# Own orders for the first and last slots of a software pipeline of four graph layers

## The reference

```python
x = layernorm(x + edge(x))       # relu(A[i] + (C - A)[j]) with A = C - b = adj @ x, maximum over i: in effect a shift by relu(max(adj @ x) + b)
x = layernorm(x + gat(x))        # h = x W; scores leaky_relu(s1 + s2) * adj; softmax; att @ h + beta h; elu
x = layernorm(x + gcn(x))        # (adj @ x) W2 + bias
x = layernorm(x + attention(x))  # 8 heads of 64, q, k, v with biases, masked where adj == 0, softmax
```

## Time and profile before

| | us |
|---|---|
| median of 3 runs (2518.87 to 2520.77) | 2519.57 |
| the profiled execution, its own time | 2517.59 |
| its span, first to last instruction | 2515.7 |
| PE busy in the span | 2433.5 (97%) |
| DVE busy | 2216.3 (88%) |
| POOL busy | 1477.2 (59%) |
| ACT busy | 1333.6 (53%) |

### The profile page before, as it was taken

One profiled execution on the slowest core, in us unless ns is written; L12 is line 12 of the kernel. 1 busy time (PEld: TensorE's weight loads), 2 busy tenths in 40 slices (PEclk: granted clock), 3 DMA queues, 4 the chain that ended last, 5 costly groups with the idle time before them and its releaser, 6 DMA issues. The chain is left out here.

```text
span 2515.7 us, 55083 instructions
## 1 busy us (share of the span) xinstructions
PE 2433.5 (97%) x15509; PEld 2071.0 (82%) x15509; DVE 2216.3 (88%) x6934; ACT 1333.6 (53%) x4104; POOL 1477.2 (59%) x1806
## 2 busy tenths in 40 slices
PE   4899999999999999999999999999999999999995
PEld 3688888888888888888888888888888888888874
DVE  6889889989889889889889989999999999999974
ACT  3355555555555555555555555555555555555543
POOL 5655566566565565566566566566566565665641
PEclk9899999999999999999999999999999999999997
DMA  4265665665665665666666666666666666666564
GB/s 130 48 138 132 142 146 130 143 144 133 142 143 137 141 143 137 142 139 138 141 139 139 140 139 141 139 138 142 138 138 142 138 139 141 139 141 138 126 137 103
DMA packets 1375069, 341.01 MB, mean 136 GB/s; under 512 B 1078576, under 2 KB 1339312, under 8 KB 1375024
## 3 DMA queue, kind: packets, MB, share of 16 engines
q1 hardware_dynamic: 1375024, 340.47, 59.4%
HBM read 173.35 MB, written 166.99 MB: 135 GB/s over the span
## 5 line engine op out<-in xcount | busy, mean ns | idle before, releaser
L928 PE MATMUL rot<-w_hi,y_hi 128*128 128x512 f32 x1024 | 416.0, 406 | 2.8 <-DVE y_lo L842 2.1
L930 PE MATMUL rot<-w_hi,y_lo 128*128 128x512 f32 x1024 | 403.8, 394 | 0.0
L929 PE MATMUL rot<-w_lo,y_hi 128*128 128x512 f32 x1024 | 402.3, 393 | 0.0
L517 ACT ACTIVATE probs<-score,sc_nmax 128x128 f32<-128x128 f32 x1024 | 362.3, 370 | 27.3 <-DVE sc_nmax L682 24.2
L387 POOL TENSOR_TENSOR ve<-mv,eps_col 128x1 f32<-128x1 f32 (+1 forms) x448 | 130.9, 292 | 342.6 <-DVE mv L674 245.9
L420 POOL TENSOR_TENSOR x2b<-x,bias 128x512 f32<-128x512 f32 x128 | 166.1, 1298 | 264.1 <-DVE x L786 264.1
L682 DVE CUSTOM_DVE_ANT_0 score<-score,mask 128x128 f32<-128x128 f32 x1024 | 259.7, 315 | 1.3 <-PE score L1027 1.3
L704 DVE CUSTOM_DVE_ANT_0 dot_tmp<-x,u 128x512 bf16<-128x512 f32 x256 | 244.9, 992 | 11.9 <-ACT x L626 7.4
L430 POOL TENSOR_SCALAR e<-e 128x512 f32<-128x512 f32 x128 | 246.5, 1925 | 13.6 <-ACT e L577 13.6
L395 POOL TENSOR_TENSOR rs<-ve,half_neg 128x1 f32<-128x1 f32 (+1 forms) x448 | 249.5, 571 | 0.6
L415 POOL TENSOR_TENSOR x<-x,o_norm 128x512 f32<-128x512 f32 x128 | 165.8, 1295 | 141.4 <-DVE o_norm L740 141.4
(11 more groups left out here) (129 smaller groups left out, 7057.4 us busy)
## 6 DMA issues: line engine op xcount, KB each, us to landing
pt_hbm<-probs SPq DMA_DIRECT2D x508, 128.0 KB, 2.8
probs_t<-pt_hbm SPq DMA_DIRECT2D x127, 512.0 KB, 4.0
x_in<-in_x SPq DMA_DIRECT2D x128, 256.0 KB, 4.0
xt_hbm<-x_b SPq DMA_DIRECT2D x512, 64.0 KB, 2.3
xt_f<-xt_hbm SPq DMA_DIRECT2D x128, 256.0 KB, 2.8
out_x<-x SPq DMA_DIRECT2D x128, 256.0 KB, 2.5
ot_hbm<-o_t SPq DMA_DIRECT2D x508, 64.0 KB, 1.9
o_norm<-ot_hbm SPq DMA_DIRECT2D x127, 256.0 KB, 2.7
```

The costliest lines, as they stand in the source:

```text
L517: ins = act.activation(probs[:, 0, c, t, :], score_tile(c, g, h), ACT.Exp, bias=sc_nmax[:, c, t:t + 1], scale=-1.0, accum_out=sc_sum[:, pa ...
L928: pe.matmul(outp, lh, rh, start=first, stop=False)
L929: pe.matmul(outp, lh, rl, start=False, stop=False)
L930: return pe.matmul(outp, ll, rh, start=False, stop=last)
```

## The change

`slots` now takes three orders for each engine: `fill` for slots 0 to 7, `emit` (as before in slots 8 to 127, but for the points below) and `drain` for slots 128 to 135.

```diff
-def slots(eng, emit):
-    for s in range(WARM):
+def slots(eng, fill, emit, drain):
+    for s in range(FILL):
+        fill(Slot(s - s % BUFS, s % BUFS))
+    for s in range(FILL, WARM):
         emit(Slot(s - s % BUFS, s % BUFS))
     with eng.Fori(0, (LOOP_END - WARM) // BUFS) as turn:
...
-    for s in range(LOOP_END, SLOTS):
+    for s in range(LOOP_END, GRAPHS):
         emit(Slot(s - s % BUFS, s % BUFS))
+    for s in range(GRAPHS, SLOTS):
+        drain(Slot(s - s % BUFS, s % BUFS))
```

**Weights' lower parts on DVE**, in slots 1 to 5, in four instructions of 128 x 512 spread over the slot:

```diff
+            def lower_weight(slot, k):
+                n = slot.number() - 1
+                dve.wait_ge(w_hi_done, n + 1)
+                return dve.tensor_tensor(weights[w_order[n]][1][:, k, :], stage[n][:, k, :],
+                                         weights[w_order[n]][0][:, k, :].bitcast(F32), ALU.subtract)
```

**Edge product** of slots 0 to 7 in one plain fp32 product, without ACT's x_hi and POOL's x_lo:

```diff
+            def edge_product(slot):
+                buf = slot.buf(L_EDGE, 4)
+                if slot.fills():
+                    pe.wait_ge(x_loaded[buf], (slot.graph(L_EDGE) - buf) * 4 + 16)
...
+                if slot.fills():
+                    return pe.matmul(rot[0][:, :], adj_t[:, :], x_in[:, buf, :], start=True, stop=True)
+                return three(rot[0][:, :], (adj_t_hi[:, :], adj_t_lo[:, :]), (x_hi[:, :], x_lo[:, :]), True, True)
```

**Drain order of PE**, with PV's wait and PV now apart (the products between them cut to their names):

```diff
+            def drain(slot):
+                if slot.on(L_PV):
+                    if slot.last(L_PV):
...
+                    else:
+                        slot.wait(pe, pt_in, L_PV, each=16)
+                if slot.on(L_GAT):
...
+                if slot.on(L_QK) and not slot.last(L_QK):
...
+                    projection(q_bank, "wq", slot).then_inc(q_mm, 1)
+                if slot.on(L_ATT):
...
+                if slot.on(L_QK) and not slot.last(L_QK):
...
+                    projection(k_bank, "wk", slot).then_inc(k_mm, 1)
+                if slot.last(L_QK - 1):
...
+                    projection(late_q_bank, "wq", slot.after(), True).then_inc(q_mm, 1)
...
+                    ins.then_inc(score_mm, 1)
+                if slot.last(L_QK - 1):
...
+                    projection(late_k_bank, "wk", slot.after(), True).then_inc(k_mm, 1)
+                if slot.on(L_PV):
+                    first = slot.buf(L_PV, BUFS) // GROUP * GROUP
...
+                    ins.then_inc(pv_mm, 1)
```

More of the change, by code:

```diff
@@ L56 @@
 SLOTS = GRAPHS + L_OUT
+WEIGHTS = 5
 class Slot:
@@ L327, in emit @@
                     buf = slot.buf(L_LOAD, 4)
-                    slot.wait(sp, x_lo_done, L_LOAD, 4)
+                    slot.wait(sp, edge_mm, L_LOAD, 4)
                     slot.wait(sp, x1_done, L_LOAD, 4)
                     load(slot.graph(L_LOAD), buf)
[L333 to L338, removed]
                 if slot.on(L_TR):
@@ L360, in emit @@
                                      x4[:, first + g, :]).then_inc(out_stored[g], 16)
-            slots(sp, emit)
+            slots(sp, fill, emit, drain)
             for g in range(GROUP):
@@ L459, in emit @@
                         .then_inc(out_shift_done, GROUP)
-                if slot.on(L_EDGE) and not slot.on(L_QK):
-                    add_eps(slot, "0", L_EDGE)
-                    power(slot, "0", L_EDGE)
-                low_x(Slot(slot.base, slot.offset + 1))
+                if slot.after().on(L_EDGE) and not slot.after().fills():
+                    low_x(Slot(slot.base, slot.offset + 1))
                 if slot.on(L_GAT):
@@ L478, in emit @@
                     power(slot, "2", L_GCN)
-                for n in range(len(w_order)):
-                    if slot.first(n):
-                        split_weight(n)
                 if slot.on(L_V):
@@ L497, in _ @@
+            slots(pool, fill, emit, drain)
         @block.scalar
@@ L551, in emit @@
                 if slot.on(L_QK):
+                    if slot.first(L_QK):
+                        act.wait_ge(const_in, 16 * 4)
                     slot.wait(act, q_mm, L_QK)
@@ L595, in emit @@
                         half.then_inc(half_exp, 1)
-                round_x(Slot(slot.base, slot.offset + 1))
-                for n in range(1, len(w_order)):
-                    if slot.first(n - 1):
-                        split_weight(n)
+                if slot.after().on(L_EDGE) and not slot.after().fills():
+                    round_x(Slot(slot.base, slot.offset + 1))
                 if slot.on(L_QK):
@@ L638, in _ @@
+            slots(act, fill, emit, drain)
         @block.vector
@@ L923, in _ @@
+            slots(dve, fill, emit, drain)
         @block.tensor
@@ L952, in _, with projection @@
             y2 = [a[:, :].rearrange("p (k n) -> p k n", k=KC) for a in (y2_hi, y2_lo)]
-            def projection(banks, w, slot):
+            def projection(banks, w, slot, late=False):
                 w_hi, w_lo = weights[w]
@@ L960, in projection @@
                     cols = slice(chunk * P, (chunk + 1) * P)
-                    if c == 1:
+                    if c == 1 and not late:
                         slot.wait(pe, score_exp, L_QK, 1)
@@ L1067, in emit @@
                 if slot.on(L_EDGE):
[L1069 to L1081 removed]
+                    edge_product(slot).then_inc(edge_mm, 1)
                 if slot.on(L_ATT):
@@ L1105 @@
+            slots(pe, fill, emit, drain)
 _INS = ["x", "adj", "L0_gnn_b", "L1_gnn_W", "L1_gnn_a", "L1_gnn_beta", "L2_gnn_weight", "L2_gnn_bias",
```

1024 lines of the change are left out of this document (952 added, 72 removed).

## The result

The changed kernel takes 2581.2 us (2577.72 to 2585.82) where the kernel before takes 2519.57: 1.0245 times as long, with a 95% interval of 1.0233 to 1.0258. The prediction was 2587 (2552 to 2606), slower. The profiled execution takes 2577.72 with a span of 2575.9, so it is to be set against the span of 2515.7: +60.2. One more run of the kernel before took 2733.55 and is left out of its median as a slow execution.

What follows compares the result with a forecast made beforehand. PE bounds the middle, so only the ends move: drain +73.0 from the uncovered HBM round trip, fill -5.5, sum +67.5 on 2517.59 gives 2585.1; with 1.98 for the median 2587 us, range 2552 to 2606.

Steps and rivals of the forecast that it cites:

- slot 128's first product: Drain: PE's first product of slot 128 waits for the probs_t landing, 2405.3 instead of 2394.11, +11.2 us.
- A: Drain, slots 128 to 132: products ahead of the scores, no longer beside the round trip, 56.4 us in sum.
- B: Drain: the way from the scores to the next block transpose, 46.3 us in sum (bounds 40 and 51).
- C: Drain: round trip through HBM from block transpose to landing, five times 11.1, 55.5 us (bounds 52 and 61).
- slot 133's start to the end: End of the drain: from slot 133's scores to the end of the span, 25.2 us against 22.45 before.
- +2.1 a slot: Drain, products ahead of the scores: PE starts at the lower clock after some 9 us of waiting (bounds 1 and 4).
- The late projection: Drain: a gain, as slot 133 loses 7.6 us of products and joins and slot 132 pays 0.9 + 2.9.
- the faster rival: Drain: the front wait holds nothing, late projection nets about -6.5 and the fill -5.5, 2507.6 us; chance 0.08.
- The fill: Slots 0 to 7: -8.8 + 2.9 + 0.4 = -5.5 us, between -11 and +2.
- the middle is bound by PE and the change leaves it alone: Slots 8 to 127: order kept, PE busy 2292.0 of 2294.8 us from slot 6 to 127, only the ends can move.
- Paid, but less: Drain: the wait costs less, the clock returns at once and DVE's order lengthens nothing, 2567 us; chance 0.12.
- The fill gives nothing: Fill: POOL's e1 holds DVE's two-input subtractions, three holds take 5.5 back, drain as forecast, 2592.5 us; chance 0.10.

Runs made afterwards that it cites:

- before_wait_early: The kernel before with only PE's wait for pt_in moved to the head of slots 128 to 133: 2587.48 us, ratio 1.027.
- wait_late: The changed kernel with PV's wait directly ahead of PV again, plus a wait for the last exponentials ahead of slot 133's scores: 2520.39 us, ratio 1.001.
- warm: The changed kernel with 38 products that nobody reads ahead of each of the six waits for pt_in: 2575.96 us, ratio 1.0228.
- fill_early: The changed kernel's fill with the drain of the kernel before, its wait for probs_t moved to the head of slots 128 to 133: 2577.56 us, ratio 1.0239.
- late_dve: wait_late with VectorE's drain list of the kernel before, the two late joins placed behind o_t: 2512.58 us, ratio 0.9977.
- fill_only: The changed kernel's fill, with the drain of the kernel before on all five engines: 2507.95 us, ratio 0.9958.
- edge3: fill_only with the edge product of slots 0 to 7 in three passes again, x_hi on ScalarE and x_lo on GpSimd: 2518.72 us, ratio 1.0001.
- fill_att2: fill_only with, in the fill, nmax straight behind the maximum, att_p ahead of e1 and att_n ahead of y2's lower part: 2505.15 us, ratio 0.9947.
- orders_only: fill_only with the weights' lower parts on GpSimd and the three-pass edge product again, leaving the fill's orders and DMA list: 2521.82 us, ratio 1.0007.
- pool_weights: fill_only with the weights' lower parts on GpSimd again, one instruction at the end of slots 0 to 4: 2523.0 us, ratio 1.0016.

## Why the prediction was right, and where its terms were off

**What bounds the kernel, and where the loss would be.** Right in mechanism and size: from the moment when PE is ready for slot 128 to the end pass 193.2 us in place of 121.6, +71.6, where +73.0 was forecast. The median came out 6 below the forecast, and the fill accounts for that. `before_wait_early` shows that the wait at the slot's head does it by itself, and `wait_late` that its undoing takes 61 away.

**Drain, term by term**, read from the changed kernel's timeline (first products as above; scores at 2406.01, 2439.79, 2471.61, 2499.90 and 2530.54; block transposes at 2417.88, 2449.05, 2480.27, 2508.99 and 2541.86):

| term | forecast | measured |
|---|---|---|
| slot 128's first product | +11.2 | +11.1 |
| A, products ahead of the scores | 12.4, 12.4, 10.7, 10.3, 10.6 = 56.4 | 12.3, 12.4, 11.3, 9.6, 10.2 = 55.8 |
| B, scores to the next block transpose | 9.5, 9.5, 8.1, 8.1, 11.1 = 46.3 | 11.9, 9.3, 8.7, 9.1, 11.3 = 50.2 |
| C, block transpose to landing | 5 x 11.1 = 55.5 | 9.6, 11.3, 10.0, 11.3, 9.6 = 51.7 |
| slot 133's start to the end | 25.2 | 24.5 |

The measured sums are rounded after adding. B was 4 short and C 4 long; that these two cancelled was luck. C's forecast was a mean over slots in which PE's own work ran beside the DMAs; why it is shorter here I didn't test. B was short in slot 128 above all: "o_t, the residual, y2's lower part and `att_n` stand ahead of the first minima" is what the trace shows, but these wait for PV, so the first minimum comes 5.0 behind the scores (2411.02) and not at once:

```profile
2408.88 0.65 DVE L1702 SCALAR_TENSOR_TENSOR r<-rot,x 128x512 f32<-128x512 f32 x1
...
2409.46 0.67 DVE L1708 TENSOR_TENSOR y_lo<-rot,y_hi 128x512 fp32r<-128x512 f32 x1
...
2410.23 0.86 DVE L1717 SCALAR_TENSOR_TENSOR att_n<-att_p,att_inv,beta_i 128x128 f32<-128x128 f32 x1
...
2411.02 0.28 DVE L1132 CUSTOM_DVE_ANT_0 score<-score,mask 128x128 f32<-128x128 f32 x1
```

The clock's share inside A, "+2.1 a slot", was nearly right: `warm` takes 1.8, 2.0, 2.5 and 1.3 off slots 128 to 131, 1.9 on average. That the whole kernel gains less than 10.5 from the clock is due to slot 132, which `warm` leaves at the lower clock, and to B and C, which give 1.8 back.

**The late projection.** I wrote "the late projection itself is a gain", 7.6 against 0.9 + 2.9, and in the faster rival "net about -6.5". Under the early wait, where the products of slot 133 would lie behind the landing, the traces agree with the first: the changed kernel is 3.0 shorter than `fill_early` from slot 132's first product to the end, though the other engines' orders are in that difference too. The second failed. Under the late wait the 7.6 us were the cover of a round trip, `late_dve` shows the wait of 9.0 in their place, and from PV of slot 131 to the end it is 1.5 longer than `fill_only`. The rival's 2507.6 was reached (2507.95), but without the late projection and with twice the fill.

**The fill** was mis-sized: -5.5 forecast, and PE is ready for slot 128 at 2382.68 in place of 2394.11, -11.4; by the times of `fill_only` it is -10.9. By marks:

| mark | forecast | measured |
|---|---|---|
| y1's lower part in slot 2 | -6.6 | -7.8 (29.92) |
| the same in slot 4 | -10.9 | -9.2 (60.35) |
| PE's first product of slot 6 | -8.8 | -11.9 (87.39) |
| stalls for `att_n` in slots 6 and 7 | +1.6, +1.3 | +1.38, +1.29 |
| slot 8's first product | -5.5 | -8.6 (127.39 in place of 135.96) |
| slots 10, 12 and 14 | 0 | -2.8 |

These marks are of one trace each. In the seven traces with the change's fill, slot 6 starts between 87.39 and 90.39, and PE is ready for slot 128 between 2382.68 and 2384.48, so the gain at slot 6 is 8.9 to 11.9 and only its sign and rough size can be read from a mark.

Three things were missing. The first: from slot 4 to slot 6 I let `att_n`'s delay and nothing else act, while the three-pass product and its x_lo are gone as well. `edge3` prices them at 10.8, where I had written that this time "was not on the path".

The second is PE's clock in the fill, which no term of mine has. In slots 4 and 5 of the kernel before 19 products of the GAT weight product run at the lower clock, in the changed kernel none. By an estimate from their distance, 0.43 in place of 0.23, that is 3.8 us; how much of it was on the path no run shows. It also makes most of the spread above: in three of the seven traces slot 5's product runs at full clock, in four 7 or 8 of its parts don't, and there slot 5 lasts some 2 us longer. These are the lines from the changed kernel and from `wait_late`, whose fills are the same code:

```profile
76.76 0.39 PE L1796 MATMUL rot<-w_hi,y_hi 128*128 128x512 f32 x1
...
76.69 0.63 PE L1796 MATMUL rot<-w_hi,y_hi 128*128 128x512 f32 x1
```

The third: "the middle is bound by PE and the change leaves it alone" was not quite so. In the kernel before, PV waits for its landing in three early slots, with these lines in the timeline:

```profile
185.82 1.09 PE L1058 MATMUL rot<-probs_t,v_sb 128*64 128x128 f32 x16 [0.85 <-DMA probs_t<-pt_hbm]
...
224.53 1.09 PE L1058 MATMUL rot<-probs_t,v_sb 128*64 128x128 f32 x16 [1.05 <-DMA probs_t<-pt_hbm]
...
263.07 1.09 PE L1058 MATMUL rot<-probs_t,v_sb 128*64 128x128 f32 x16 [0.88 <-DMA probs_t<-pt_hbm]
```

In the changed kernel, in `fill_only` and in `fill_att2` there are none; in `edge3` and `orders_only`, whose first slots have the three-pass product, they are there again with 2.2 and 2.5 in sum, in `pool_weights` one of 0.5 is left. What in the first eight slots shifts the scatter's landing in slot 10 is open.

**The rivals.** *Paid, but less* (2567): its C of 52 was met, its A of 46 and B of 43 were not, and the clock did not come back at once. *Faster: the wait holds nothing*: the 11.1 us ahead of slot 128's first product rule it out. *The fill gives nothing*: three VectorE pieces were indeed held by GpSimd's residual sum, but they are the third piece of a weight, 0.7 to 1.0 longer each (1.67 at 38.90, 1.35 at 67.87, 1.34 at 82.05). Behind the last two VectorE soon stands idle for PE (0.3 at 70.72 and 84.87), so they cost nothing; behind the first it works without a pause up to slot 3's y1 lower part, so that one may have cost up to 1.0.

On that hold the Trainium skill ("SBUF — State Buffer", Who interferes with whom) says that a two-input VectorE instruction contends with a GpSimd one that reads SBUF, and calls the shared port pair an exclusive lock, though it spells out the block for the whole instruction only for the two-port modes. The trace agrees with the lock for the dot product of `pool_weights`: it ends 0.54 behind GpSimd's end, about its own 0.68.

On the wait, the Trainium skill's advice to wait late ("DMA: Bandwidth & Descriptors", Rules for kernel authors) is borne out with a number: 61 us for one wait that stands some ten us of products too early, in six slots.

## What to carry to other kernels

When a wait is moved, write down what stands behind it in that engine's list, and ask for each transfer which work has covered it until now; a slot whose products are taken away may only have its wait laid bare. Two edits that free the same engine have to be measured together as well as apart: here two moves that by themselves brought nothing clear of noise made 14 us together. And a round trip of some 10 us that the products beside it had covered adds its whole length to the slot, 30 to 34 us in place of 18.8, as soon as its wait stands in front of them. Last, before a difference of 2 or 3 us between two traces is explained, look how far the same code lies apart in the traces at hand, and whether the clock differs.

## What the runs showed of the hardware

- GpSimd's subtraction of 128 x 2048 holds not only long VectorE instructions: the leaky relu of 128 x 128 took 3.57 beside it in place of 0.28, and `att_n` 3.75 in place of 0.35.
- The lower clock behind gaps of 9 to 13 us costs this chain little: with PE kept busy in the gaps the drain was 5.7 of 193 us shorter (1.3 to 2.5 in each of the four slots that came back to full clock), although the mean granted clock of the stretch had been 0.76.
- The same fill ran at different clocks from one execution to the next: slot 5's weight product at full clock in three traces, in part at the lower clock in four, which are 2 us longer there.
- From slot 8's first product to the end of slot 127 pass 2255.2 us in `fill_only` and `wait_late` and 2255.3 in the changed kernel, and 2258.0 or more where PV waits in the early slots. But in `late_dve`, with the same middle, it is 2253.6, so a difference of 2 us in the middle of a single trace is told from its waits and not from its length.
